# A graph network megakernel: attention weights normalized before the rows are weighed, and the fetches and moves of both attention layers placed anew

## The reference, cut to what matters

```python
def gat_conv(x, src, dst, edge_attr, W, att_src, att_dst, W_edge, att_edge, bias):
    xh = (x @ W).reshape(N, H, C)                    # H = 4 heads of C = 32
    ...
    alpha = leaky_relu(a_src[src_f] + a_dst[dst_f] + a_edge, 0.2)
    m = segment_max(alpha, dst_f)
    p = exp(alpha - m[dst_f])
    s = segment_sum(p, dst_f)
    alpha = p / (s[dst_f] + 1e-16)
    out = segment_sum(xh[src_f] * alpha[..., None], dst_f)
    return out.reshape(N, H * C) + bias
```

## Time and profile before

| | |
|---|---|
| median of three runs | 5932.02 us (5927.41 to 5933.96) |
| the profiled execution | 5926.84 us |
| its span, first to last instruction | 5924.7 us |
| mean granted TensorE clock | 0.789 |
| TensorE busy | 3305.5 us (56%) |
| VectorE busy | 3795.5 us (64%) |
| ScalarE busy | 2891.4 us (49%) |
| GpSimd busy | 3713.9 us (63%) |

### The profile page before, as it was taken

One profiled execution on the slowest core, in us unless ns is written; L12 is line 12 of the kernel. 1 busy time (PEld: TensorE's weight loads), 2 busy tenths in 40 slices (PEclk: granted clock), 3 DMA queues, 4 the chain that ended last, 5 costly groups with the idle time before them and its releaser, 6 DMA issues. The chain is left out here.

```text
span 5924.7 us, 68941 instructions
## 1 busy us (share of the span) xinstructions
PE 3305.5 (56%) x17186; PEld 2363.5 (40%) x17363; DVE 3795.5 (64%) x10364; ACT 2891.4 (49%) x6936; POOL 3713.9 (63%) x3700
## 2 busy tenths in 40 slices
PE   0534994727330000777777758888688854354443
PEld 0433662727320000444444436665466634343232
DVE  7349994539491995888888856665366645454332
ACT  0964994413100221777777747777477743232110
POOL 0664776757675676745536456764677537676776
PEclk9867997757665555899999979999899976656666
DMA  2223773637321674435546445553344447564333
GB/s 67 82 95 123 243 244 121 197 87 191 83 51 44 167 188 121 128 116 117 122 105 132 111 153 189 190 185 139 92 154 147 141 159 245 171 201 138 125 120 100
DMA packets 512325, 826.98 MB, mean 140 GB/s; under 512 B 108999, under 2 KB 193843, under 8 KB 510796
## 3 DMA queue, kind: packets, MB, share of 16 engines
q1 hardware_dynamic: 396011, 629.55, 32.4%
q0 software_dynamic: 115936, 193.21, 14.8%
HBM read 382.25 MB, written 452.03 MB: 141 GB/s over the span
## 5 line engine op out<-in xcount | busy, mean ns | idle before, releaser
L2972 POOL DMA_INDIRECT gcn_ring<-GT,gcn_index x588 | 585.0, 995 | 199.1 <-issue 169.5
L3073 DVE SCALAR_TENSOR_TENSOR gcn_acc<-gcn_acc,cont,gcn_ring 128x128 f32<-128x128 f32 x588 | 203.8, 347 | 560.8 <-DMA gcn_ring<-GT,gcn_index 559.7
L482 POOL DMA_INDIRECT J<-packed,sort_place x392 | 442.6, 1129 | 155.3 <-issue 121.5
L1513 POOL DMA_INDIRECT light_ring<-C,light_s_u x392 | 375.9, 959 | 260.4 <-DVE light_acc L1556 152.3
L3155 PE MATMUL gcn_psA<-ident,gcn_h 128*128 128x128 f32 x588 | 155.4, 416 | 594.8 <-DVE gcn_h L3076 594.4
L3122 ACT ACTIVATE gcn_hT<-gcn_psA 128x512 f32<-128x512 f32 x147 | 87.8, 597 | 692.5 <-PE gcn_psA L3155 692.3
L3155 PEld LDWEIGHTS gcn_psA<-ident,gcn_h 128*128 128x128 f32 x588 | 100.3, 208 | 633.7 <-DVE gcn_h L3076 633.7
L1358 ACT ACTIVATE tail_h<-tail_x,tail_nmr,tail_std 128x128 f32<-128x128 f32 x784 | 320.8, 484 | 10.5 <-DVE tail_nmr L1289 10.5
L2225 POOL DMA_INDIRECT out<-source_x,source_own_u x196 | 193.7, 988 | 192.5 <-DVE source_x L2305 146.8
L1407 PE MATMUL tail_psT<-ident,tail_h 128*128 128x128 f32 x784 | 132.1, 294 | 267.8 <-ACT tail_h L1358 267.8
L473 POOL DMA_INDIRECT got_s<-TAB,src_u x196 | 191.7, 978 | 133.7 <-POOLq L1606 69.9
(11 more groups left out here) (631 smaller groups left out, 12422.7 us busy)
## 6 DMA issues: line engine op xcount, KB each, us to landing
T<-front_t SPq DMA_DIRECT2D x196, 272.0 KB
C<-light_acc SPq DMA_DIRECT2D x147, 256.0 KB, 2.3
source_c<-C SPq DMA_DIRECT2D x147, 256.0 KB
GT<-source_r SPq DMA_DIRECT2D x147, 256.0 KB, 2.1
gcn_own<-GT SPq DMA_DIRECT2D x147, 256.0 KB
RC<-gcn_own SPq DMA_DIRECT2D x147, 256.0 KB
RG<-gat_rows SPq DMA_DIRECT2D x98, 264.0 KB
front_x<-in_x SPq DMA_DIRECT2D x98, 256.0 KB
```

Source lines behind the costliest of these rows:

```text
L482: nc.gpsimd.indirect_dma_start(out=table, out_offset=bass.IndirectOffsetOnAxis(ap=index[:, c:c + 1], axis=0), in_=rows[:, c, :], in_offset ...
L1513: nc.gpsimd.indirect_dma_start(out=ring[:, n % RING, j, :], out_offset=None, in_=tables[h], in_offset=bass.IndirectOffsetOnAxis(ap=index[: ...
L2972: nc.gpsimd.indirect_dma_start(out=ring[:, n % RING, j, :], out_offset=None, in_=net.GT[i], in_offset=bass.IndirectOffsetOnAxis(ap=index[: ...
L3073: nc.vector.scalar_tensor_tensor(out=acc[:, n % 2, j, :], in0=before, scalar=net.cont[:, c:c + 1], in1=ring[:, n % RING, j, :], op0=ALU.mu ...
```

## The change

- The weights are divided before the rows are weighed. The preparation of each layer scans `alpha` for its sums, carries them over partitions by TensorE, adds `pself`, takes the reciprocal of 128 x 784 numbers, multiplies `pself` by it, spreads it from the owners over their runs (`owner_scan`, `owner_carry`), and multiplies `alpha` by it. The copy of `alpha` into `Y` goes. The chain and RG are 128 wide. `rows` keeps only the product with `pself` and the addition, and the patch loses its reciprocal and product.
- Layer 1's first 152 columns are fetched beside the own projection, the other 44 at the start of the attention block, and nothing waits for their landing at a block's end. VectorE waits for all of them at the score addition (`v.wait_ge(rows_in, 16 * T)`). Layer 2's first 112 are fetched beside the high digit, the other 84 in its attention block.
- Layer 1's move has no pacing. 180 scatters stand behind the fetches, and 16 behind the patch's two small fetches, with the reload of `packed`.
- Layer 2's move begins with the scatters of eight groups ahead of the row loop, and stays eight groups ahead in it. The reload stands behind the patch's three small fetches.

```diff
-    net.AD1, net.RG = dram("AD1", (EP, WA)), dram("RG", (EP, D + H))
+    net.AD1, net.RG = dram("AD1", (EP, WA)), dram("RG", (EP, D))
...
+FETCHED_1, FETCHED_2 = 152, 112
+MOVED_LATE, MOVE_AHEAD = 16, 8
...
             def fetch_sources(pool, projected):
-                gather_static(nc, net.T1, src_u, Y, rows1_in, passed=beside(pool, projected, S, NG))
-                pool.wait_ge(rows1_in, 16 * T)
+                gather_static(nc, net.T1, src_u, Y, rows1_in, range(FETCHED_1), passed=beside(pool, projected, S, NG))
...
-            def move_and_turn_back(pool, projected):
-                scatter_static(nc, net.J1, place, packed, moved, passed=beside(pool, projected, S, NG))
+            def fetch_rest_and_move(pool):
+                gather_static(nc, net.T1, src_u, Y, rows1_in, range(FETCHED_1, T))
+                scatter_static(nc, net.J1, place, packed, moved, range(T - MOVED_LATE))
+
+            def move_rest_and_turn_back(pool):
+                scatter_static(nc, net.J1, place, packed, moved, range(T - MOVED_LATE, T))
                 pool.wait_ge(moved, 16 * T)
                 pool.dma_start(packed[:, :, :], as_columns(net.J1)).then_inc(turned_back, 16)
                 pool.wait_ge(turned_back, 16)
-            phase_attend_rows(nc, net, 0, Y, move_and_turn_back, lambda pool, m: None)
+            phase_attend_rows(nc, net, 0, Y, rows1_in, fetch_rest_and_move, None, move_rest_and_turn_back)
...
             def fetch_rows(pool, counted):
-                gather_static(nc, net.T2, q_u, Y, rows2_in, passed=beside(pool, counted, HU // 2, T // HU))
-                pool.wait_ge(rows2_in, 16 * T)
+                gather_static(nc, net.T2, q_u, Y, rows2_in, range(FETCHED_2), passed=beside(pool, counted, HU // 2, T // HU))
...
+            def fetch_rest_and_begin(pool):
+                gather_static(nc, net.T2, q_u, Y, rows2_in, range(FETCHED_2, T))
+                scatter_static(nc, net.J2, place, packed, moved2, range(MOVE_AHEAD * S))
+
             def move(pool, m):
-                scatter_static(nc, net.J2, place, packed, moved2, range(m * S, (m + 1) * S))
-                if m == NG - 1:
-                    pool.wait_ge(moved2, 16 * T)
-                    pool.dma_start(packed[:, :, :], as_columns(net.J2)).then_inc(loaded2, 16)
-                    pool.wait_ge(loaded2, 16)
-            phase_attend_rows(nc, net, 1, Y, lambda pool, projected: None, move)
+                if m + MOVE_AHEAD < NG:
+                    scatter_static(nc, net.J2, place, packed, moved2, range((m + MOVE_AHEAD) * S, (m + MOVE_AHEAD + 1) * S))
+
+            def turn_back(pool):
+                pool.wait_ge(moved2, 16 * T)
+                pool.dma_start(packed[:, :, :], as_columns(net.J2)).then_inc(loaded2, 16)
+                pool.wait_ge(loaded2, 16)
+            phase_attend_rows(nc, net, 1, Y, rows2_in, fetch_rest_and_begin, move, turn_back)
...
-def phase_attend_rows(nc, net, layer, Y, on_pool, each_group_pool):
+def phase_attend_rows(nc, net, layer, Y, rows_in, on_pool, each_group_pool, at_last):
...
-        xh, inv = sb("xh", [P, XR, S, WA]), sb("inv", [P, 2, S, H])
-        fix_row, fix_xh, fix_out = sb("fix_row", [P, W_]), sb("fix_xh", [P, WA]), sb("fix_out", [P, WA])
-        at, at_n, p_at, fix_inv = sb("fix_at", [P, 1], U32), sb("fix_at_n", [P, 1], U32), sb("p_at", [P, H]), sb("fix_inv", [P, H])
+        xh = sb("xh", [P, XR, S, WA])
+        fix_row, fix_xh, fix_out = sb("fix_row", [P, D]), sb("fix_xh", [P, WA]), sb("fix_out", [P, WA])
+        at, at_n, p_at = sb("fix_at", [P, 1], U32), sb("fix_at_n", [P, 1], U32), sb("p_at", [P, H])
...
-                on_pool(pool, xh2_done if first_layer else None)
-                for m in range(NG):
-                    each_group_pool(pool, m)
-                    if not first_layer:
+                on_pool(pool)
+                if not first_layer:
+                    for m in range(NG):
+                        each_group_pool(pool, m)
...
                 if first_layer:
                     nc.gpsimd.indirect_dma_start(out=fix_xh[:, :], out_offset=None, in_=net.AD1,
                                                  in_offset=bass.IndirectOffsetOnAxis(ap=at[:, 0:1], axis=0)).then_inc(fetched, 16)
+                    at_last(pool)
                     for k in range(OUT):
                         pool.wait_ge(t2_out[k], 16 * slots_used(OUT, k))
                     pool.wait_ge(fix_ready, 1)
...
                                                  in_offset=bass.IndirectOffsetOnAxis(ap=at[:, 0:1], axis=0)).then_inc(fetched, 16)
+                    at_last(pool)
                     for k in range(len(spare)):
...
-                        after(sp, num_made, m, XR)
+                        after(sp, gat_made, m, XR)
...
-                        sp.dma_start(rows_of(net.RG, n), block_of(n, W_)).then_inc(raw_out[n % OUT], 16)
+                        sp.dma_start(rows_of(net.RG, n), block_of(n, D)).then_inc(raw_out[n % OUT], 16)
...
                 scores_in = Y[:, :, D:W_].rearrange("p t h -> p h t")
+                v.wait_ge(rows_in, 16 * T)
                 link(nc.vector.tensor_tensor(alpha[:, :, :], scores_in, of_owner[:, :, :], ALU.add))
...
+                den, inv = m_, m_
                 v.wait_ge(a_step, 2)
-                link(nc.vector.tensor_copy(scores_in, alpha[:, :, :]))
+                for h in range(H):
+                    last = nc.vector.tensor_tensor_scan(den[:, h, :], net.cont[:, :], alpha[:, h, :], 0.0, ALU.mult, ALU.add)
+                link(last)
+                value["sums"] = steps[0]
+                v.wait_ge(t_step, 4)
+                link(nc.vector.tensor_copy(net.carry[:, 0:H], psF[:, 408:408 + H]))
+                for h in range(H):
+                    last = nc.vector.scalar_tensor_tensor(out=den[:, h, :], in0=net.first[:, :], scalar=net.carry[:, h:h + 1],
+                                                          in1=den[:, h, :], op0=ALU.mult, op1=ALU.add)
+                link(last)
+                link(nc.vector.scalar_tensor_tensor(out=den[:, :, :], in0=den[:, :, :], scalar=1e-16, in1=net.pself[:, :, :], op0=ALU.add, op1=ALU.add))
+                link(nc.vector.reciprocal(inv[:, :, :], den[:, :, :]))
+                link(nc.vector.tensor_tensor(net.pself[:, :, :], net.pself[:, :, :], inv[:, :, :], ALU.mult))
+                owner_scan(nc, link, net, inv[:, :, :], of_owner)
+                value["inverses"] = steps[0]
+                v.wait_ge(t_step, 5)
+                owner_carry(nc, link, net, psF[:, 412:412 + H], of_owner)
+                link(nc.vector.tensor_tensor(alpha[:, :, :], alpha[:, :, :], of_owner[:, :, :], ALU.mult))
...
-                        nc.vector.scalar_tensor_tensor(out=Y[:, c, 0:W_], in0=Y[:, c - 1, 0:W_], scalar=net.cont[:, c:c + 1], in1=Y[:, c, 0:W_],
+                        nc.vector.scalar_tensor_tensor(out=Y[:, c, 0:D], in0=Y[:, c - 1, 0:D], scalar=net.cont[:, c:c + 1], in1=Y[:, c, 0:D],
...
-                    nc.vector.scalar_tensor_tensor(out=inv[:, m % 2, :, :], in0=Y[:, m * S:(m + 1) * S, D:W_], scalar=1e-16, in1=of_self,
-                                                   op0=ALU.add, op1=ALU.add).then_inc(den_made, 1)
                     v.wait_ge(xh_in[m % XR], 16 * (m // XR + 1))
                     nc.vector.tensor_tensor(heads(mine), heads(mine), of_self.unsqueeze(3).to_broadcast([P, S, H, CH]), ALU.mult).then_inc(self_made, 1)
-                    v.wait_ge(den_made, m + 1)
-                    nc.vector.reciprocal(inv[:, m % 2, :, :], inv[:, m % 2, :, :]).then_inc(inv_made, 1)
                     v.wait_ge(self_made, m + 1)
-                    nc.vector.tensor_tensor(got, got, mine, ALU.add).then_inc(num_made, 1)
-                    v.wait_ge(num_made, m + 1)
-                    v.wait_ge(inv_made, m + 1)
-                    nc.vector.tensor_tensor(heads(got), heads(got), inv[:, m % 2, :, :].unsqueeze(3).to_broadcast([P, S, H, CH]), ALU.mult).then_inc(gat_made, 1)
+                    nc.vector.tensor_tensor(got, got, mine, ALU.add).then_inc(gat_made, 1)
...
-                fix(nc.vector.tensor_tensor(fix_row[:, :], fix_row[:, :], psF[:, 0:W_], ALU.add))
-                fix(nc.vector.scalar_tensor_tensor(out=fix_inv[:, :], in0=fix_row[:, D:W_], scalar=1e-16, in1=p_at[:, :], op0=ALU.add, op1=ALU.add))
-                fix(nc.vector.reciprocal(fix_inv[:, :], fix_inv[:, :]))
+                fix(nc.vector.tensor_tensor(fix_row[:, :], fix_row[:, :], psF[:, 0:D], ALU.add))
                 by_head = lambda t: t[:, 0:D].rearrange("p (h c) -> p h c", h=H)
                 fix(nc.vector.tensor_tensor(by_head(fix_xh), by_head(fix_xh), p_at[:, :].unsqueeze(2).to_broadcast([P, H, CH]), ALU.mult))
                 fix(nc.vector.tensor_tensor(fix_row[:, 0:D], fix_row[:, 0:D], fix_xh[:, 0:D], ALU.add))
-                fix(nc.vector.tensor_tensor(by_head(fix_row), by_head(fix_row), fix_inv[:, :].unsqueeze(2).to_broadcast([P, H, CH]), ALU.mult))
...
```

(8 more changed lines are left out.)

## The result

The changed kernel took 5841.71 us (median of 4 runs, 5833.66 to 5843.20) against 5931.48 (4 runs, 5927.41 to 5933.96) of the kernel before on the same chip: a ratio of 0.985, 95% interval 0.983 to 0.986. The forecast was 5841. Its profiled execution took 5842.58 us, 1.7 of them around the span.

The account below looks back on a forecast made before the run. GpSimd's order was taken to set layer 1's end, with GpSimd and VectorE both full in layer 2. Gains of 42.5 and 44 us, 86.5 together, gave 5840.3, plus 1 toward the median: 5841 us, range 5808 to 5874.

Parts of the forecast that it names:

- What bounds a layer: Both layers: GpSimd sets layer 1's end from first fetch to last scatter; in layer 2's loop GpSimd and VectorE are full.
- GpSimd then binds: Layer 2's row loop: GpSimd's own 6.9 us a group exceeds VectorE's 6.3, so 40 groups take 276 us.
- The handover: Block ends before attention: layer 1's block starts at 1233.9 us, layer 2's 7.8 us behind fetch 112; remaining fetches follow inside.
- The preparation: Score addition to first weighing, each layer: 17 us longer than 24.24, bounds 13 to 18, including a 5.1 us reciprocal.
- This gain is hidden: Layer 1's rows: VectorE's period falls from 4.31 to 3.5 us, but GpSimd ends later, so it does not show.
- Layer 1: GpSimd's unpaced scatters finish at 1546.5 us and T2's patch starts at 1575 instead of 1617, gaining 42 us.
- Layer 2: Start, loop and end of layer 2: HD's patch at 2274 instead of 2318.22 us, gaining 44 us.
- The tail: Layer 2's last eight groups, without scatters: VectorE about three groups ahead, the other five at 6.3 us, last add at 2265.
- Scatters as fast as alone: Rival, both layers: 1.28 us a scatter everywhere, 117 us gained, 5811 us; chance 0.10.
- Layer 2 in its old step of 7.2: Rival, layer 2's loop: GpSimd's own work keeps 7.2 us a group, 13 us less gain, 5854 us; chance 0.18.
- Fetches did not suffer beside the preparation: Rival claimed they would: 0.2 us for each of 128, plus 4 us per layer at block ends, 5874 us; chance 0.06.
- Scatters at 1.7: Slower rival, both layers: VectorE holds up GpSimd's DMA instructions, 1.75 us a scatter costs 129 us, 5970 us; chance 0.04.

Follow-up runs that it names:

- the placement by itself: Changed kernel with weights divided behind the rows as in the kernel before, fetches and moves as changed; 5877.25 us, ratio 0.992 to the kernel before.
- The paced version: Changed kernel with layer 1's 180 early scatters paced on TensorE again; 5877.20 us, ratio 0.992 to the kernel before.
- the two-input passes: Changed kernel plus 62 idle VectorE passes of 128x512 behind layer 1's rows: 18 two-input, 26 copies, 18 reductions; single run 5848.12 us.

## Why the prediction was right

**What bounds a layer** was read rightly in layer 1, and the runs show it: the division by itself, which shortens VectorE's loop there, made the layer 4.7 us longer, and the placement by itself, which shortens GpSimd's order, made it 36.4 shorter. In layer 2 it is shown for the start, where the eight groups ahead took the wait of 46.03 us away. In the loop of before it was GpSimd that waited, 0.32 us in each step, so the division alone gained there; and in the changed kernel's loop neither engine waits. "GpSimd then binds" is half of it.

**The handover.** Block starts were forecast for 1233.9 and, shifted, 1748.0; they came at 1235.4 and 1748.9. The own projection itself began 2.2 us later in this execution than before, which covers the first difference; SyncE's end set it, as forecast. At the second the drain did, with the fetches in flight, which the prediction had only as an outer bound: 9.9 us stand there where it took 7.8, and the fetches had ended 1.2 earlier than forecast.

**The preparation.** +17 was forecast, 41.2 - 24.24 = 17.0 measured; the reciprocal, extrapolated over four times its largest row, 5.1 against 5.05. VectorE waited 48.9 and 99.4 us for the scores' rows (forecast 47 and 98).

**Layer 1.** Period 3.5 against 3.48, VectorE done at about 1510 (1508), no wait for TensorE. The 1.131 us for a scatter beside the rows was too long (1.084), which is 5.6 us over 120 of them and within the margin; the patch came at 1574.3 (1575). The paced version prices the missing pauses at 40 us. "This gain is hidden", said of the shorter rows, was wrong in part: the placement alone shows 8.5 us of it, through scatters that are shorter and beside the loop for fewer groups, not through VectorE's end.

**Layer 2** gained 46.4 where 44 stood, from two errors that cancel in part; so close a figure is luck. The step was forecast as 6.9 and was (2184.64 - 1915.72)/40 = 6.72 on the mean, pauses included, 7 us less over 40 groups. The term mis-sized is the scatter, 1.131 taken and 1.057 measured, which is (0.074 x 4) x 40 = 12 us, less the pauses. The tail was forecast with VectorE three groups ahead and free a tenth of the time: "GpSimd then binds". It was one group ahead, since with the stall of 1.18 its own step is as long as GpSimd's; from add 40 to add 48 passed 34.1 us instead of 29.5, 5 us more. With the h1 additions on VectorE that stall is gone and so is the step of 6.6.

**The rivals.** Scatters as fast as alone: 1.084 and 1.057 beside the loops, 0.989 behind them, and the two-input passes, 1.168 against 1.019, show a cause. Layer 2 in its old step of 7.2 is what the placement alone does; it needed the longer loop of VectorE. Fetches did not suffer beside the preparation: from the block's first instruction to the score addition it took 59.0 us in layer 1 (58.4 forecast) and 109.4 in layer 2 (110.2). Scatters at 1.7 existed, four in each preparation, but the mean over all 392 was 1.073, with its 0.31 of issue 1.385 a scatter.

**Slips in the working.** The bound for scatters at 1.55 beside VectorE is 30 us by the prediction's own steps (141 of the 180 out when the rows end, 39 at 1.28 behind them), not 33. The mean issue step of before is 507.5/353 = 1.44 by the earlier trace rows, not 1.42. Layer 1's gain is worked out as 42 and enters the sum as 42.5. None of them moves the forecast by more than 0.5.

**Open.** Why the three later scatters of a step in layer 2 take 0.97 and the first 1.26, with VectorE busy throughout, was not separated; so which passes, and at which point of a scatter, hold it up is not shown. A version with the additions on VectorE and fewer groups ahead was not run.

## What to carry to other kernels

When two engines look full, take the one whose instructions stand in a fixed order from the layer's first input to its last output, and count that order; a shorter loop on the other is worth little until the order is freed, and then more than it was alone (here 10 us of the two layers, then 33). Small work handed to GpSimd to relieve VectorE has to be priced at both ends: an add of 1.28 us there held VectorE up by 1.18 and would have cost it 0.69. A head start by n groups saves its wait at the beginning and gives back part of it over the last n groups, which run at the other engine's pace.

## What the runs showed of the hardware

The drain of GpSimd at a block's end depends on what is in flight. With all fetches landed it took 6.83 us. In the changed kernel, whose last fetches are in flight, these are the drains of the own projection and of the block ahead of layer 2 (ns three times, then the recorded start, twice):

```profile
...
L1765 POOLq DRAIN  x1: 18580/18580/18580, 1213.0 to 1213.0; - x1
...
L705 POOLq DRAIN  x1: 24617/24617/24617, 1723.6 to 1723.6; - x1
...
```

Their ends are 1231.6 and 1748.2, so 3.6 us behind the last fetch's end (1227.96) and 9.2 behind it (1739.05); the recorded starts lie ahead of the last fetches. In the first SyncE ended later (1234.3) and set the block's end, in the second this drain did. Three of the other kernels (the placement alone, the additions on VectorE, no scatter behind the small fetches) repeat both: 3.2 to 3.8 us behind the last fetch in the first, 9.2 to 9.3 in the second. What makes the two differ is open.

GpSimd's addition costs VectorE about one us wherever it falls: in the changed kernel's loop the sum takes 1.87 instead of 0.69, and in its tail, where the addition stands beside the chain, the chain takes 2.54 instead of 1.55.

A reciprocal on VectorE costs about 6.4 ns an element of a partition (5.05 us for 784) where a sum of two inputs costs 1.24 (0.97).
